# Scatter-adds four steps behind their gathers, table scatters one tile a step, low pieces in two operations

## What is computed

```
scores = einsum('td,ed->te', xf, gate_w); probs = softmax(scores)
weights, idx = top_k(probs, 2); weights = weights / sum(weights)
x1 = silu(einsum('td,efd->tef', xf, w1)); x3 = einsum('td,efd->tef', xf, w3)
out_all = einsum('tef,edf->ted', x1 * x3, w2)
x = x + tanh(g_ffn[0]) * sum over the row's two experts of weight * out_all
```

## Time and profile before

| | |
|---|---|
| three runs | 1417.0, 1421.34, 1421.36 us; median 1421.34 us |
| the profiled execution | 1407.95 us, span 1406.2 us |
| TensorE busy | 1297.4 us, 92% of the span |
| VectorE, ScalarE, GpSimd busy | 911.0, 761.5, 627.0 us |
| mean granted TensorE clock | 0.945 of full speed |
| the blocks | from 165.3 us (first transposes) to 510.0 us (last add's issue) |

### The profile page before, as it was taken

How to read it: one execution, slowest core, us unless ns; L and a number is a source line. 1 busy time by engine, 2 the same in 40 slices (tenths; PEclk the granted TensorE clock), 3 DMA queues, 4 the chain that set the end, 5 groups by cost and what they waited for, 6 DMA issues and landing times.

```text
span 1406.2 us, 29217 instructions
## 1 busy us (share of the span) xinstructions
PE 1297.4 (92%) x9858; PEld 975.7 (69%) x9859; DVE 911.0 (65%) x2128; ACT 761.5 (54%) x2315; POOL 627.0 (45%) x664
## 2 busy tenths in 40 slices
PE   7966699999999999899999985899999999999997
PEld 3755588879999968788888773356656666566555
DVE  2887664565555577778776885777776555566651
ACT  3775332432332365988887752655645555555551
POOL 2177678666666540454444433133333333333113
PEclk8675599999999999999999996999999999999999
DMA  4657444654334351100210103244444444444322
GB/s 146 213 163 184 96 50 56 122 109 67 63 60 64 63 142 40 39 32 32 91 39 24 34 31 93 106 120 121 121 121 124 150 158 148 126 130 129 108 45 31
DMA packets 81546, 133.17 MB, mean 95 GB/s; under 512 B 24662, under 2 KB 71260, under 8 KB 76316
## 3 DMA queue, kind: packets, MB, share of 16 engines
q1 hardware_dynamic: 51132, 93.92, 20.1%
q0 software_dynamic: 29312, 37.57, 16.5%
q10 hardware_dynamic: 992, 0.27, 0.1%
HBM read 95.08 MB, written 36.65 MB: 94 GB/s over the span
## 4 chain that ended last, share of the span: by engine, by line
PE 70%; DVE 10%; DMA 6%; issue 5%; POOL 5%; ACT 2%; SPq 0%; POOLq 0%; ACTq 0%; DVEq 0%
PE psG L124 5%; PE psG L126 5%; PE psG L125 5%; PE psU L124 5%; PE psU L126 5%; PE psU L125 5%; PE psYb L124 4%; PE psYb L125 4%; PE psYb L126 4%; DMA stage<-in_w 3%; PE psP L1798 2%; PE psS L124 2%; PE psS L125 2%; PE psS L126 2%; PE psOL L126 2%
## 5 line engine op out<-in xcount | busy, mean ns | idle before, releaser
L2118 POOL DMA_INDIRECT out_x<-yo,gidx x64 | 100.2, 1566 | 324.0 <-ACT yo L2220 310.8
L2268 DVE SCALAR_TENSOR_TENSOR hid<-psU,sil 128x512 f32<-128x512 f32 x128 | 88.4, 691 | 167.2 <-ACT sil L2209 166.7
L980 POOL DMA_INDIRECT x_rows<-yo,tabs x78 | 124.7, 1599 | 91.7 <-ACT yo L1052 68.0
L1720 ACT ACTIVATE pr<-psS,mx 128x77 f32<-128x77 f32 x512 | 158.8, 359 | 5.2 <-DVE mx L1889 5.2
L2209 ACT ACTIVATE sil<-psG 128x512 f32<-128x512 f32 x128 | 76.4, 597 | 118.1 <-PE psU L126 118.1
L126 PE MATMUL psYb<-W1dh,hl 128*128 128x256 f16 x512 | 139.6, 273 | 0.0
L125 PE MATMUL psYb<-W1dl,hh 128*128 128x256 f16 x512 | 139.6, 273 | 0.0
L124 PE MATMUL psYb<-W1dh,hh 128*128 128x256 f16 x512 | 139.6, 273 | 0.0
L1079 DVE SCALAR_TENSOR_TENSOR hid<-psU,sil 128x512 f32<-128x512 f32 x78 | 53.8, 690 | 127.3 <-ACT sil L1043 127.2
L1720 ACT ACTIVATION_READ_ACCUMULATOR pr<-psS,mx 128x1 f32 x512 | 123.6, 242 | 0.0
L1043 ACT ACTIVATE sil<-psG 128x512 f32<-128x512 f32 x78 | 46.5, 596 | 134.2 <-PE psU L126 132.2
(11 more groups left out here) (407 smaller groups left out, 4331.1 us busy)
## 6 DMA issues: line engine op xcount, KB each, us to landing
w1u<-in_w SPq DMA_DIRECT2D x16, 2048.0 KB, 7.4
w1d<-in_w SPq DMA_DIRECT2D x16, 1024.0 KB, 9.7
stage<-in_w SPq DMA_DIRECT2D x8, 1536.0 KB, 8.9
X<-in_x SPq DMA_DIRECT2D x8, 512.0 KB, 8.6
n_rows<-xc SPq DMA_DIRECT2D x8, 512.0 KB, 9.0
x_rows<-X SPq DMA_DIRECT2D x8, 512.0 KB, 10.2
X<-x_rows SPq DMA_DIRECT2D x8, 512.0 KB, 8.0
out_x<-X SPq DMA_DIRECT2D x32, 128.0 KB, 1.7
```

Of the source, the lines that this page charges most:

```text
L980: pool.indirect_dma_start(x1_rows[:, :], bass.IndirectOffsetOnAxis(tabs[:, j, n, 0:1], 0), yo[:, par, n, :], None, compute_op=ALU.add).the ...
L1720: ins = act.activation(pr1[:, par, h * LK:(h + 1) * LK], psS1[:, q, i * LK:(i + 1) * LK], ACT.Exp, bias=mx1[:, h:h + 1], scale=1.0 / (SX * ...
L2118: pool.indirect_dma_start(out_rows[:, :], bass.IndirectOffsetOnAxis(gidx[:, half, col:col + 1], 0), yo1[:, j % 2, n, :], None, compute_op= ...
L2268: dve.scalar_tensor_tensor(hid1[:, f % 2, :], psU1[f % 2][:], SH / (SX * SW), sil1[:, f % 2, :], ALU.mult, ALU.mult).then_inc(d_hid, 1)
```

## The change

Adds lag their gathers by four steps instead of three. The ten late tiles go one to a step (1 to 10) instead of two at step 2 and the last at step 9. The low half of each piece is made by two VectorE operations in two steps: part 0 at step 11+i in the old place, part 1 at step 12+i between `rows_low` and the second `hidden`. SP's wait counts both parts.

```
+        def parts(i):
+            name, _, cols, _ = PIECES[i]
+            n = tiles_of[name]
+            return [(P, 0, n * cols // 2), (P, n * cols // 2, n * cols)] if n == HP else regions(i)
...
-                wait(sp, b_w1l, i)
+                wait(sp, b_w1l, 2 * i)
...
-        LATE_SCATTERS = {1: (2,), 2: (3, 4), 3: (5,), 4: (6,), 5: (7,), 6: (8,), 7: (9,), 8: (10,), 9: (11,)}
+        LATE_SCATTERS = {n - 1: (n,) for n in range(2, 12)}
...
-            pipeline(pool, NB0, BDEPTH, [(0, gather), (0, late_scatter), (3, add)], straight=True)
+            pipeline(pool, NB0, BDEPTH + 1, [(0, gather), (0, late_scatter), (4, add)], straight=True)
...
+            def low_piece(n):
+                def run(j, par):
...
+                    dve.wait_ge(b_w1h, i + 1)
+                    rows, c0_, c1_ = parts(i)[n]
+                    dve.scalar_tensor_tensor(split1[name][1][0:rows, c0_:c1_], raw1[0:rows, c0_:c1_], scale,
+                                             split1[name][0][0:rows, c0_:c1_], ALU.mult, ALU.subtract).then_inc(b_w1l, 1)
...
-            pipeline(dve, NB0, PEEL, [(2, hidden(0)), (1, rows_low), (2, hidden(1)), (1, low_piece), (2, late_list)])
+            pipeline(dve, NB0, PEEL + 1, [(2, hidden(0)), (1, rows_low), (2, low_piece(1)), (2, hidden(1)), (1, low_piece(0)), (2, late_list)])
```

More of the change, by code:

```diff
@@ L1086, in hidden @@
                 return run
[L1088 to L1097, removed]
+            def low_piece(n):
+                def run(j, par):
+                    i = piece_of(j)
+                    if i is None:
+                        return
+                    name, _, _, scale = PIECES[i]
+                    dve.wait_ge(b_w1h, i + 1)
+                    rows, c0_, c1_ = parts(i)[n]
+                    dve.scalar_tensor_tensor(split1[name][1][0:rows, c0_:c1_], raw1[0:rows, c0_:c1_], scale,
+                                             split1[name][0][0:rows, c0_:c1_], ALU.mult, ALU.subtract).then_inc(b_w1l, 1)
+                return run
             late = Chain(dve, s_blk, EARLY_STEPS, 1)
@@ L1250, in prep_tensor @@
             pe.wait_ge(b_w1h, len(PIECES))
-            pe.wait_ge(b_w1l, len(PIECES))
+            pe.wait_ge(b_w1l, 2 * len(PIECES))
             for turn, (name, psum) in enumerate((("wk1", psM), ("wv1", psN))):
```

## The result

The changed kernel is slower: 1429.14 us median against 1418.14 us in the same comparison (14 runs each), ratio 1.0072, interval 1.0061 to 1.0082. The forecast was 1428.6 us, with a range of 1419.5 to 1433. Its profiled execution took 1429.82 us, with a span of 1428.0 us. A pair from one chip follows with the experiments (e1 and e4).

What follows compares the result with a forecast made beforehand. GpSimd's gather issue, then the loop of piece load, high half, low half and next request were taken to bound the kernel. T(16) 5.7 us later plus 1.6 for the clock made 7.3 us slower: 1428.6 us, range 1419.5 to 1433.

Steps and rivals of the forecast that it cites:

- What bounds the kernel: Before block 16: late gathers lose 3.7 us in T(5) to T(11), the piece loop 5.9 us in T(11) to T(16).
- Adds a step later: GpSimd's row: one gather fits its idle gap, every gather comes 9.1 us earlier, T(11) at 253.3, a gain of 3.7 us.
- First request at T(11) + 3.8, the gain spent at once: SP's first piece request: at 257.1 us, where it was 257.05, so the 3.7 us gained are spent at once.
- The loop: Pieces 1 to 3: high half to next request 6.77 us against 4.26, the whole loop 12.7 to 12.9 us.
- Clock: TensorE behind the last idle gap: the granted clock falls and costs 1.6 us, bounds 0 and 4.
- Three times 4.5 us idle: TensorE between 270 and 308 us: idle about 4.5 us three times, from a 12.8 us loop against 8.29 us of work.
- R1: Piece loads get 1.4 to 1.5 us shorter with earlier gathers, so no change: 1421 to 1422.6 us; chance 0.16.
- R2: VectorE's second low operation isn't felt, the loop keeps 10.4 us: 3.7 us gained, 1417.6 us; chance 0.05.
- R3: Waits for `bx`, not pieces, set T(11) to T(16); both stretches run at 8.29 us: -9.6 us, 1411.7; chance 0.07.
- Sum forecast: Whole kernel: 5.7 us later at T(16) plus 1.6 us for the clock, 7.3 us slower, median 1428.6 us.

Runs made afterwards that it cites:

- e1: The kernel before, not edited, profiled and timed once more: 1406.47 us median, ratio 0.9988 to the kernel before.
- e4: The changed kernel, not edited, profiled and timed once more: 1415.11 us median, ratio 1.0053 to the kernel before.
- e2: The kernel before with only the GpSimd part: adds four steps behind, late tiles one to a step, low pieces as before; ratio 0.9970.
- e7: The kernel before with the adds four steps behind and nothing else; ratio 0.9970.
- e5: The changed kernel with part 1 of the low piece at the head of VectorE's step, ahead of `hidden` and `rows_low`; ratio 0.9978 to the kernel before.
- e6: The changed kernel with part 1 of the low piece one function later, behind the second `hidden`; ratio 1.0114 to the kernel before.
- e3: The changed kernel with the two GpSimd lines of before, so only the low pieces in two operations; ratio 1.0079 to the kernel before.
- e10: The changed kernel with each piece's load, high and low half in two parts, low operations at the old place, loads counted apart; 1401.88 us, ratio 0.9941 to before.
- e11: The kernel before, not edited, run once more in a later comparison: 1409.87 us, ratio 0.9990 to the kernel before.
- e9: The kernel before with the late tiles one to a step and nothing else, adds still three steps behind; ratio 1.0014.
- e12: The changed kernel, not edited, run once more in a later comparison: 1419.36 us, ratio 1.0050 to the kernel before.

## Why the prediction was right

*What bounds the kernel* was right in both stretches. GpSimd's issue set T(5) to T(11) (e2, e7), the loop of pieces T(11) to T(16) (e5, e6), and what T(16) gains or loses arrives at the end: e2, e3 and e10 moved T(16) by -4, +10.5 and -10.5 us from the mean of e1 and e11, and the whole time by -4.2, +11.1 and -8.3 (from the ratio and the kernel before's median of that comparison). What is missing for e10, 2.2 us, lies within its interval of 2.5 us to either side.

*Adds a step later:* T(2) to T(11) forecast at 253.3 - 178.66 = 74.6 us, found 74.7. That the tiles' new spread costs and gives nothing beside the lag was right (e7), but alone it is no help (e9).

*First request at T(11) + 3.8, the gain spent at once:* in e4 it came at 258.32, T(11) + 3.8.

*The loop:* from the high half to the next request 6.77 us forecast, 6.7 to 7.0 found in e4. The load was taken at 5.9 to 6.2 us; in e4 it was 6.8, 5.5, 6.8 and 6.3. That term was a little small, by 0.3 us a piece in the mean of e4 and 0.1 in e12, and e9 shows it isn't a constant at all. T(11) to T(16) was forecast at 56.8 without the clock; it is 58.2 in e4, and 58.9 - 1.5 = 57.4 in e12.

*Clock:* 1.6 us forecast behind the last gap. By the time from the last `up` to T(16), less 2.63, it was 1.7 us in the profile after (325.66 - 321.36 = 4.30), 1.7 in e3 and in e6, 1.5 in e12 and 0 in e4. So it is a matter of the execution, and in four of five traces it came as forecast. "Three times 4.5 us idle" had the wrong shape: TensorE's gaps ahead of `up` were 2.60, 2.12, 5.07 and 1.82 us in e4. Behind the first and the third the clock fell, the work took longer and filled part of the loop, and the next gap was short. The length of a gap alone doesn't tell whether the clock falls: behind 2.15 us in e7 it did, behind 2.28 us in e12 it didn't. The Trainium skill (TensorE: Matmul & The Clock Gate, "What's actually happening") has activity as what releases the throttle. The trace of e12 agrees: TensorE works without a gap from 313.21 us on, and from 318 us on the clock is at 1.00 again.

*Rivals.* R1 didn't come about: 1024 KB never took 4.5 us, the shortest was 5.65 (wq in e9). The fit from the Trainium skill (DMA: Bandwidth & Descriptors, "Anatomy of one DMA"), which by its words is for a DMA from GpSimd and would give 4.4 us (an estimate), isn't met by any load of a piece of that size from SP here. R2 was tried as e5: it needs part 1 in another place. R3 fell with e2, where the gathers were a step earlier and T(11) to T(16) still took 47.9 us.

*The size.* Sum forecast 7.3 us; 7.5 and 7.1 us by the ratios of e4 and e12, 10 by the first comparison. There the median came within 0.6 us of the forecast 1428.6, and that is luck: the three runs it starts from had a median of 1421.34, 3.2 us above that of the fourteen, and the difference of the medians was 11.0 us, 3.7 above the sum. Its profile takes 67.73 us from T(4) to T(11), where e4 takes 58.08. That stretch, 9.65 us longer, is the one with the pauses, in one execution; that they explain the larger ratio is argued, not shown.

## What to carry to other kernels

A buffer that is refilled piece by piece makes a loop through every engine it visits; when its period exceeds the step, each function put ahead of the operation that frees it costs its full duration once per piece, however idle that engine is (here 2.5 us for `hidden` and `rows_low` together, 1.8 more for the second `hidden` in e6). Before an operation is split to smooth an engine's row, look at what waits for its last part. A consumer may lag its producer by a step more at no cost (e7) where the queue's issue is the bound and the engine had an idle gap ahead of the first consumer.

## What the runs showed that I had not expected

Loads of one size differ with their place: wv, 768 KB, took 6.2, 6.6, 5.5, 5.3 and 5.2 us in the traces of before, e1, e4, e12 and e9. The Trainium skill (DMA: Bandwidth & Descriptors, "Queues, rings and completion order") says that each DMA engine alternates between its queues packet by packet; that fits loads which share their six microseconds with gathers and adds, though no run here isolates it.

TensorE paused for 0.2 to 0.9 us at a time inside its matmul groups, some fourteen times, in one of fourteen traces, with no wait shown there and the granted clock at 1.00. The cause stays open.
